# Down products with a wait of their own bank, and padding rows, tile loads, last choices and the first projection in another order

## The reference

```
V = exp(dA_log[:, :, None] * l);  K = 2.0 * einsum('chn,hnl->chl', Ct, V).real      # features
u = layernorm(x, gamma, beta);  gates = einsum('btd,de->bte', u, W_in) + b_in
h = (1 - sigmoid(delta)) * h + sigmoid(delta) * b_proj;  y = h * tanh(c_proj)       # scan over t
out = y @ W_out + b_out + x @ W_skip + b_skip
scores = softmax(x @ gate_w);  topk_w, topk_idx = top_k(scores, 2)
g = silu(einsum('td,edh->teh', x, w_gate)) * einsum('td,edh->teh', x, w_up)
routed = einsum('teh,ehd,te->td', g, w_down, comb)
shared = silu(x @ sw_gate) * (x @ sw_up) @ sw_down                                   # HS = 704
```

## Time and profile before

| | |
|---|---|
| median of 3 runs | 1255.14 us (1252.26 to 1257.32) |
| profiled execution | 1257.11 us, its span 1255.4 us |
| PE | 1066.7 us busy (85%), 7869 matmuls |
| DVE | 813.4 us (65%) |
| ACT, POOL | 347.8 us (28%), 383.5 us (31%) |
| DMA | 183.57 MB, mean 146 GB/s |
| mean granted clock of PE | 0.931 |

### The profile page before, as it was taken

The page is one execution under the profiler, slowest core; times in us unless marked ns, Lnnn a source line. Parts: engine busy times, 40 slices in busy tenths (PEclk is TensorE's granted clock), DMA queues, the critical chain, the costliest instruction groups (busy, mean ns, idle before and its releaser), DMA issues.

```text
span 1255.4 us, 26490 instructions
## 1 busy us (share of the span) xinstructions
PE 1066.7 (85%) x7869; PEld 700.4 (56%) x7870; DVE 813.4 (65%) x2123; ACT 347.8 (28%) x658; POOL 383.5 (31%) x352
## 2 busy tenths in 40 slices
PE   2056798999999999999999994759899999999995
PEld 2035566657666776567665761525455555555552
DVE  7965877888888878888788663324344444444443
ACT  5312332343344333433344321101111111111110
POOL 1010220222122211221122210115455555555554
PEclk8556798999999999999999998889999999999998
DMA  7323245444544545354534589458998788778885
GB/s 249 99 44 94 68 139 133 125 143 160 155 123 134 170 137 167 98 166 151 169 102 148 164 260 351 141 109 177 191 226 137 129 136 131 128 128 134 131 131 71
DMA packets 311150, 183.57 MB, mean 146 GB/s; under 512 B 261218, under 2 KB 280034, under 8 KB 309044
## 3 DMA queue, kind: packets, MB, share of 16 engines
q1 hardware_dynamic: 294548, 137.45, 44.4%
q0 software_dynamic: 15504, 36.46, 14.4%
q10 hardware_dynamic: 1040, 8.91, 1.7%
HBM read 53.40 MB, written 79.73 MB: 106 GB/s over the span
## 4 chain that ended last, share of the span: by engine, by line
PE 60%; DVE 15%; SPq 6%; issue 4%; DMA 3%; POOLq 0%; ACT 0%; DVEq 0%; POOL 0%
PE bank L994 22%; PE bank L1144 9%; PE bank L1134 9%; PE bank L1135 9%; PE bank L1069 5%; PE bank L1008 4%; DVE wexp L1327 3%; SPq L799 2%; DVE h L1507 2%; DVE wexp L1343 2%; DVE stat L1510 1%; DVE h L1508 1%; DVE x2w L1558 1%; DMA mixed<-mixed 1%; DVE h L1520 1%
## 5 line engine op out<-in xcount | busy, mean ns | idle before, releaser
L994 PE MATMUL bank<-wexp 128*128 128x256 f16 (+2 forms) x3252 | 409.2, 287 | 7.0 <-DVE yT L1528 4.1
L994 PEld LDWEIGHTS bank<-wexp 128*128 128x128 f16 x3252 | 310.6, 99 | 86.3 <-issue 12.1
L1134 PE MATMUL bank<-wexp,rows_in 128*128 x852 | 256.4, 314 | 10.8 <-issue 3.6
L1135 PE MATMUL bank<-wexp,rows_in 128*128 x852 | 255.9, 313 | 0.0
L1069 PE MATMUL bank<-wexp 128*128 128x512 f16 x495 | 126.6, 414 | 40.5 <-DVE h L1520 40.5
L924 POOL TENSOR_TENSOR inv<-var,power 128x4 f32<-128x4 f32 x17 | 29.2, 1716 | 409.9 <-DVE var L1500 409.9
L972 POOL DMA_INDIRECT out<-x2w,rows_in x71 | 113.4, 1597 | 120.5 <-DMA out<-x2w,rows_in 83.7
L960 POOL TENSOR_TENSOR ex<-base,ld 128x8 f32<-128x8 f32 x71 | 120.1, 1692 | 84.6 <-DVE ld L1630 68.4
L1651 DVE SCALAR_TENSOR_TENSOR mixed<-bank,mixed 128x352 f32<-128x352 f32 x71 | 37.2, 525 | 165.3 <-ACT mixed L1284 115.2
L1008 PE MATMUL bank<-wexp 64*128 64x64 f32 x1024 | 72.0, 299 | 65.3 <-DVE wexp L1332 65.3
L1134 PEld LDWEIGHTS bank<-wexp,rows_in 128*128 128x128 f16 x852 | 83.3, 98 | 68.5 <-issue 28.3
(11 more groups left out here) (281 smaller groups left out, 1245.8 us busy)
## 6 DMA issues: line engine op xcount, KB each, us to landing
w_halves<-rows_in SPq DMA_DIRECT2D x16, 704.0 KB, 4.9
wexp<-w_halves ACTq DMA_DIRECT2D x1, 8704.0 KB
wexp<-w_halves SPq DMA_DIRECT2D x8, 1088.0 KB
h_tok<-tokens SPq DMA_DIRECT2D x16, 512.0 KB, 3.1
mixed<-h_tok SPq DMA_DIRECT2D x32, 256.0 KB
out<-h SPq DMA_DIRECT2D x32, 256.0 KB
w_halves<-rows_in SPq DMA_DIRECT2D x16, 384.0 KB, 5.0
x_slots<-zrow SPq DMA_DIRECT2D x8, 768.0 KB, 4.8
```

Of the source, the lines that this page charges most:

```text
L994: last = MM(dst, stat_of(step, a), mov_of(step, b), start=(s_ == 0 and a + b == 0), stop=(s_ == len(steps) - 1 and a == 1))
L1134: MM(GB[:, 0:H], xT[b][:, a, c, :], wexp[:, u, o:o + H], start=s_, stop=e_)
L1135: last = MM(UB[:, 0:H], xT[b][:, a, c, :], wexp[:, u, o + H:o + 2 * H], start=s_, stop=e_)
```

## The change

- `shared_down(i)` waits for `c_dev >= n*2` for both tiles.
- The padding of an expert becomes `pad_rows(eng, e)`. At k = NCH, SP issues experts 0 to 3 where it issued all, and 4 and 5 after the turns of `x3w`; ACT issues 6 ahead of `rows_hi(k, 0)` and 7 behind it, after waits for `c_ri` and `c_pw`.
- DVE at k = NCH: `choose` before `gprod(1)`, `place` after `gprod(2)`, and the room count (`room`) directly behind it. DVE at LAST: `choose` first of all, `place` before `glow(0)`, `table(0)` before `gprod(2)`, `table(1)` after `gprod(3)`.
- PE: `ranks` after one gate/up group at LAST and after three at NCH (it was four).
- SP at LAST issues tile loads 0 to 3; the loop of loads 2 to 7 behind it is gone, and `serve(0)` to `serve(3)` issue loads 4 to 7.
- At k = 0, PE does the projection to gates (`input_project`) before `features`, and ACT its tanh (`gate_tanh`) before the token copies.

```diff
+        def pad_rows(eng, e):
+            turn = eng.value_load(roti[0:1, e:e + 1], min_val=0, max_val=P - 1)
+            row = eng.value_load(runi[0:1, e:e + 1], min_val=0, max_val=ZERO - 3 * P)
+            eng.dma_start(xs_d[bass.ds(row, 3 * P), 2 * D:XW].bitcast(I32),
+                          pads_d[e].rearrange("r q w -> (r q) w")[bass.ds(turn, 3 * P)]).then_inc(c_z, 16)
+            eng.dma_start(xs_d[bass.ds(row, 3 * P), 0:2 * D]...).then_inc(c_z, 16)
...
                         sp.wait_ge(c_ri, 1)
                         sp.wait_ge(c_pw, 64)
-                        for e in range(E):
...
+                        for e in range(4):
+                            pad_rows(sp, e)
                     if isinstance(k, int) and k == LAST:
...
-                        for b in range(2):
+                        for b in range(4):
                             load(b, b)
...
                                                    x3w[:, i, 0:2 * D]).then_inc(c_e3[i], 16)
+                    if isinstance(k, int) and k == NCH:
+                        for e in range(4, 6):
+                            pad_rows(sp, e)
...
                 iterate(sp, body)
-                for b in range(2, UNROLL):
-                    load(b, b)
...
-                    if not at_end(i + AHEAD) and not (isinstance(i, int) and i < 4):
-                        sp.wait_ge(d_ys[b % 2], halfcount(i - 4, b))
-                        apart(sp, d_sps)
+                    if not at_end(i + AHEAD):
+                        if not (isinstance(i, int) and i < 4):
+                            sp.wait_ge(d_ys[b % 2], halfcount(i - 4, b))
+                            apart(sp, d_sps)
                         load(i + AHEAD, (b + AHEAD) % UNROLL)
...
                     def shared_down(i):
                         n = k - 1
-                        at_least(pe, c_dev, n * 2 + i)
+                        at_least(pe, c_dev, n * 2)
...
-                        for m in range(4):
+                        early = 1 if isinstance(k, int) and k == LAST else 3 if isinstance(k, int) and k == NCH else 4
+                        for m in range(early):
                             gate_up_shared(m)
                         ranks()
+                        for m in range(early, 4):
+                            gate_up_shared(m)
...
+                    first_win = isinstance(k, int) and k == 0
+                    if first_win:
+                        input_project()
+                    if htok(k + 2) and not (isinstance(k, int) and k == -1):
+                        features(k)
+                    if has(k + 1) and not first_win:
+                        input_project()
...
+                    if isinstance(k, int) and k == NCH:
+                        act.wait_ge(c_ri, 1)
+                        act.wait_ge(c_pw, 64)
+                        pad_rows(act, 6)
                     if has(k):
                         rows_hi(k, 0, q)
+                    if isinstance(k, int) and k == NCH:
+                        pad_rows(act, 7)
...
+                    if first_win:
+                        gate_tanh()
                     if isinstance(k, int) and k == -1:
                         tok_out(1, 0)
...
+                    if isinstance(k, int) and k == LAST:
+                        choose(k - 1)
                     if shared:
                         gprod(k - 1, 0)
...
                     if shared:
+                        if before_last:
+                            choose(k - 1)
                         gprod(k - 1, 1)
-                        choose(k - 1)
+                        if at_last:
+                            place(k - 1)
+                        elif not before_last:
+                            choose(k - 1)
                         glow(k - 1, 0)
+                        if at_last:
+                            table(0)
                         gprod(k - 1, 2)
+                        if before_last:
+                            place(k - 1)
+                            room()
...
                         gprod(k - 1, 3)
-                        place(k - 1)
+                        if at_last:
+                            table(1)
+                        elif not before_last:
+                            place(k - 1)
```

More of the change, by code:

```diff
@@ L1091, in body, with input_project @@
                             shared_down(i)
-                    if htok(k + 2) and not (isinstance(k, int) and k == -1):
-                        features(k)
-                    if has(k + 1):
+                    def input_project():
                         n, w, nt = k + 1, cols(k + 1), tiles(k + 1)
@@ L1264, in body @@
                         tok_out(k + 2, 1)
-                    if has(k + 1):
-                        n, w = k + 1, cols(k + 1)
-                        act.wait_ge(c_gt, n + 1)
-                        at_least(act, c_yf, n)
-                        A(th[:, 0:w], BG[:, 0:w], ACT.Tanh, bias=cbh[:, 0:1], scale=0.5 * SXW)
-                        A(tc[:, 0:w], BG[:, TOK:TOK + w], ACT.Tanh, bias=cb[:, 2:3], scale=SXW).then_inc(c_th, 1)
+                    if has(k + 1) and not first_win:
+                        gate_tanh()
                     if isinstance(k, int) and k == NCH - 1:
@@ L1418, in seated, with room @@
                     STT(pads[:, :, E], pq[:, 0, 0, :], float(T + 1), pq[:, 0, 1, :], ALU.mult, ALU.add).then_inc(c_pd, 1)
+                def room():
+                    link(TT(used[:, 0, :], run[:], ecap[:], ALU.add))
+                    link(TT(cmp1[:, :, 0:TILES - 1], used[:, 0, :].rearrange("p (e o) -> p e o", o=1).broadcast_to([P, E, TILES - 1]),
+                            jf[:, 1:TILES].rearrange("p (o j) -> p o j", o=1).broadcast_to([P, E, TILES - 1]), ALU.is_ge))
+                    link(RED(used[:, 1, :], cmp1[:, :, 0:TILES - 1], AX.X, ALU.add))
+                    link(STT(roti[:], used[:, 1, :], -float(P), used[:, 0, :], ALU.mult, ALU.add))
+                    nc.vector.tensor_copy(runi[:], run[:]).then_inc(c_ri, 1)
                 def scan(n):
@@ L1567, in body @@
                         seats()
-                    if isinstance(k, int) and k == NCH:
-                        link(TT(used[:, 0, :], run[:], ecap[:], ALU.add))
-                        link(TT(cmp1[:, :, 0:TILES - 1], used[:, 0, :].rearrange("p (e o) -> p e o", o=1).broadcast_to([P, E, TILES - 1]),
-                                jf[:, 1:TILES].rearrange("p (o j) -> p o j", o=1).broadcast_to([P, E, TILES - 1]), ALU.is_ge))
-                        link(RED(used[:, 1, :], cmp1[:, :, 0:TILES - 1], AX.X, ALU.add))
-                        link(STT(roti[:], used[:, 1, :], -float(P), used[:, 0, :], ALU.mult, ALU.add))
-                        nc.vector.tensor_copy(runi[:], run[:]).then_inc(c_ri, 1)
-                    if isinstance(k, int) and k == LAST:
-                        table(0)
                     if tokens2:
@@ L1586, in body @@
                         down_out(0)
-                    if isinstance(k, int) and k == LAST:
-                        table(1)
                     if tokens2:
```

10 lines of the change are left out of this document (added).

## The result

The changed kernel takes 1215.58 us (median of 4 runs, 1209.0 to 1219.81) against 1256.23 (1252.26 to 1263.01) beside it on the same chip: ratio 0.9666, 95% interval 0.9605 to 0.9727. Predicted were 1208 us and a range of 1192 to 1231. The profiled execution took 1219.81 us, the slowest of the four; its span is 1218.1 us.

What follows compares the result with a forecast made beforehand. PE was taken as the bound in the loop, DVE close behind, with PE standing still at the turnings. Terms 20.6 + 4.3 - 2.2 + 0.8 + 17.8 + 8 = 49.3 off 1257.1 gave 1208 us, range 1192 to 1231.

Steps and rivals of the forecast that it cites:

- Step 1: Loop, `shared_down(1)`: dropping the `c_dev` wait gains 2.3 us a chunk, less clock falls in one of four; +20.6 us.
- Step 2: First chunk, k = 0: gates ahead of features bring the clock up, so features run in 3.6 us; gain 4.3 us.
- Step 3: Chunk k = 2: 3.9 us idle now before features, the clock falls, features take 7.1 us; -2.2 us.
- Step 4: Padding at k = NCH: fewer pairs ahead of the turns, so the last router's rows land 13.3 us earlier.
- Step 5: Last chunk: choices first and tables early bring the first expert product at +24.4 us instead of +28.9; 4.5 us.
- Step 6: Expert start: loads 4 to 7 behind the serves remove PE's 8.79 us stand; +8 us (3 to 12).
- A fall in every chunk: Rival, loop: the clock falls in each chunk, 2.6 us a fall, term about -3; 1231 us, chance 0.13.
- never: Rival, loop: the clock never falls, term 27.6; 1201 us, chance 0.20.
- The turnings give half: Rival, turnings: turns queue behind padding or ACT blocks; 17.8 becomes 10, 8 becomes 2; 1222 us, chance 0.15.
- The slower one: Rival, loop: features wholly at half clock in each chunk, cadence 44.35 us; 1269 us, chance 0.04.

Runs made afterwards that it cites:

- after: The changed kernel itself, with the whole change, against the kernel before; 1215.58 us, ratio 0.9666.
- the run with pads late: Changed kernel with one padding pair on SP ahead of the router rows' turn, four behind it, three on ACT behind its weight copies; 1215.54 us.
- 3.1 MB more: Changed kernel with the zero rows of the first four padding pairs written a second time, to a scratch tensor; 1222.49 us.
- 4.35 MB less: Changed kernel with ACT's expert weight load at k = NCH - 1 cut from 8 units to 4, the others following in the expert phase; 1203.77 us.
- the scan moved: Changed kernel with gates ahead of features in every chunk to the last but one, and DVE's scan ahead of `tok_e(k + 3, 4)`; 1200.15 us.

## Why the prediction was right, and where it was not

**Step 1, the bank wait: right in mechanism and frequency, the fall too cheap.** The idle before features is 0.4 to 1.0 us (0.7 predicted) and a quiet chunk 38.4 to 39.2 (38.65). The clock falls in one chunk of four, as taken; that share was a choice and not worked out, and other runs had two and four falls, so hitting it was luck in part. But a fall costs 3.4 us and not 2.6, because the features stretch at half clock and the gates behind them too (5.16 and 5.99 us, for 3.79 and 4.10). 27.6 - 3 x 3.4 = 17.4, and 17.4 was measured. That it comes out to the tenth is luck too: the mean chunk was 41.25 us before and not 40.95, and 38.95 without the falls and not 38.65, and the two cancel. The prediction gave features 3.6 us at full clock, where its own row has 3.90; after has 3.79. Its lower bound was too high: with falls of 3.4 us in every chunk the term is -13 and not "about 0" or -3, which makes that rival 1242, outside its range. By the rule of the Trainium skill (TensorE: Matmul & The Clock Gate, "A second HAM failure mode: psum-queue depth-cycling"), as the prediction applied it, every chunk would have fallen; here 9 of 12 with idle in the same range did not.

**Step 2, projection first:** 3.6 us in the pair, of 4.3, and 3.9 to 6.6 against the run that undoes it. The gates brought the clock up (6.14 us) and the features behind ran in 3.79, ending at 114.8 (113.6 predicted, in a profile that was 1.7 us late by then). After and the run with pads late gain least, for there the 128x128 products behind the gates ran slow (7.1 and 7.0 us, 5.5 in four others) after the same 0.93 us of idle.

**Step 3, k = 2:** features slow after 3.91 us of idle, as said; the loss was 1.5 us in that chunk, and 1.2 came back in the chunk ahead of it, whose gates took 5.09 and not 6.26. That gain belongs to the order at k = 0: in the two runs with features first there these gates take 6.2 and 6.3 us, and k = 1 and 2 lose 2.3 and 2.4 us, as forecast.

**Step 4, padding rows at k = NCH: the step that failed, 7.1 us and not 13.3.** Counted from chunk 15's router, I had the turns issued at +38.4 and landed at +44.4. They were issued at +40.9 and landed at +50.4: 2.6 us lost ahead of the issue, 3.5 behind it. So PE stood for 19.25 us and not for the 5 to 8 given as a sign. I saw the block in SP's issue and took the pace of the pairs behind it, 3.4 us each, as an issue cost of SP that stays; in after the last two pairs are 4.6 apart. The turn I gave the landing time of a quiet queue. Both are the queue's: with 3.1 MB more in it the wait grew by 8.0 us, with 4.35 MB less it fell by 10.8 and the last two pairs were back at 3.4. That agrees with the rule I had weighed and left out of the sum (the Trainium skill, DMA: Bandwidth & Descriptors, "Issuing engines are not separate DMA queues"): pairs on ACT are still bytes ahead of the turn, and ACT and SP stood in an issue at the same time at 743.8 us. What a count of megabytes instead of issues would have given was not worked out.

**Step 5, last chunk:** 4.0 of 4.5 (3.5 to 5.4 in the other runs with this order); PE does not wait for the tile, as stated. No run takes this order back alone.

**Step 6, expert start:** the gap went, and first product to second down product took 19.8 us (20.3 predicted). The pair shows 6.5 of 8 for the phase. Seven profiles of this code average 423.1 us, against 434.6 in the two with the old turnings: 11.5. So the term was too small, and this profiled execution hid it. It would also explain why the profile stands 4.2 us above its median. How much of the 11.5 is the order of the loads is open: putting loads 4 to 7 back cost 2.4 by the totals and 3.5 by the mean, both within the scatter. That the stores of the last chunk and the scatter meet the loads differently may be the rest; it was not tried.

**The balance.** 1257.1 less 17.4, 3.6, 0.8, 7.1, 4.0 and 11.5, plus 0.4, is 1213.1; the median is 1215.6. Against the forecast 3.2 us are missing in the loop and 6.2 at the last router, 3.5 came back in the experts, and the small terms make up the rest.

**The rivals.** A fall in every chunk and "never" are both out. "The turnings give half" (0.15) was half true: its reason, turns queued in the DMA behind padding, is what happened at the router, though not at the last chunk or the experts. The slower one needed features at half clock in each chunk; features wholly or nearly so (6.6 to 7.1 us) are seen only behind idle of 3.9 us and more, at k = -1, 1 and 2.

There is no time without the zero rows: a kernel that leaves them out was written, but 30.5% of the elements of `x_slots` stay unwritten in it. What they cost is known only from doubling and from moving them.

## What to carry to other kernels

A wait that asks for more than its own bank is found by its regularity in the list of waits, and taking it away is worth the gap less what the next, smaller gap costs: look at which work stands behind that gap, and put dense products there and weak ones later. Where SP blocks in an issue and the DMA share is at 1, count the bytes ahead of the transfer that matters; here moving small DMAs about only moved the wait, and taking bytes out of the stretch shortened it. Read a stage by marks inside the profile, and from more than one profile, for the same code differed by 8.5 us in one phase over seven profiled executions.

## What the runs showed of the hardware

- With idle of 0.4 to 1.0 us ahead of features the granted clock came down in 2 to 4 of 12 chunks (seven profiles). The length of the idle does not decide it: in six of the seven the second and the fourth of the twelve fell (idle 1.02 or 1.03, and 0.79 to 0.94 us) and the third (0.91 to 0.96) never did. Why is open. With 0.56 us ahead of dense products it was 1, 3 and 3 chunks, and 5 and 5 with the scan moved as well. Features (64x64, float32) behind the idle make a fall cost 3.4 us, dense 128x256 products 1.6.
- One issue on SP stood for 8.42 us (10.56 with the zero rows doubled) at a DMA share of 1.0 to 1.1, whichever small DMA happened to be next in line; with 4.35 MB less queued none ahead of the turn stood over 1.7, at a share of 1.02 to 1.09.
- From the first expert product to the end the same instructions took 419.0 to 427.5 us in seven profiled executions; most of the difference lies in the first 150 us. In the second 50 of them the DMA share is 1.11 to 1.19 and PE is busy 44.3 to 47.6 us.
